# Expert layer in five pieces whose first steps alternate with the last slots of the context attention

## What is computed

```python
x = _layernorm(x + _L1_xattn_ref(x, ctx_2048, mask_BxSxS2_ff0, ...))
x = _layernorm(x + _L1_ffn_ref(x, L1_ffn_router_w, L1_ffn_down_w, L1_ffn_up_w))
# _L1_ffn_ref
logits = jnp.einsum('bth,eh->bte', x, router_w)          # 8 experts
weights = jax.nn.softmax(logits, axis=-1)
top_w, top_idx = jax.lax.top_k(weights, K)               # K = 2
gate = weights * topk_mask
a = silu(jnp.einsum('bth,eih->beti', x, down_w))         # 16 per expert
out = jnp.einsum('beth,bte->bth', einsum('beti,ehi->beth', a, up_w), gate)
```

## Time and profile before

| | us |
|---|---|
| median of 3 runs | 2366.31 |
| lowest and highest | 2366.27, 2366.6 |
| span of the profiled execution | 2368.8 |
| busy in the span: PE, DVE, ACT, POOL | 2103.1, 1295.4, 1062.5, 822.0 |

### The profile page before, as it was taken

How to read it: one execution, slowest core, us unless ns; L and a number is a source line. 1 busy time by engine, 2 the same in 40 slices (tenths; PEclk the granted TensorE clock), 3 DMA queues, 4 the chain that set the end, 5 groups by cost and what they waited for, 6 DMA issues and landing times.

```text
span 2368.8 us, 37759 instructions
## 1 busy us (share of the span) xinstructions
PE 2103.1 (89%) x13655; PEld 1671.4 (71%) x13669; DVE 1295.4 (55%) x3333; ACT 1062.5 (45%) x2367; POOL 822.0 (35%) x836
## 2 busy tenths in 40 slices
PE   7899999899999978999999999969999778888764
PEld 6688888687877866877777888756555366666542
DVE  2454445544455456545456411356777676777655
ACT  3332333444444424444534222146666547777632
POOL 1753444334343322134441135264535231322100
PEclk9899999899999998999999999979999789999986
DMA  3302102012012012011110012033324210000001
GB/s 125 135 32 67 45 32 76 19 41 65 28 45 65 19 36 72 25 53 37 41 48 25 32 40 80 1 56 55 62 44 63 94 33 28 15 19 6 1 10 71
DMA packets 57879, 109.04 MB, mean 46 GB/s; under 512 B 7136, under 2 KB 35040, under 8 KB 54112
## 3 DMA queue, kind: packets, MB, share of 16 engines
q1 hardware_dynamic: 57696, 106.63, 15.8%
HBM read 86.10 MB, written 4.26 MB: 38 GB/s over the span
## 4 chain that ended last, share of the span: by engine, by line
PE 40%; DVE 10%; issue 7%; ACT 4%; POOL 2%; DMA 1%; SPq 1%; ACTq 0%; DVEq 0%; POOLq 0%
PE PS L1293 17%; PE PS L1790 3%; PE PS L1886 3%; PE PS L1309 2%; DVE st L191 2%; ACT xP L2551 1%; DVE aM L2026 1%; PE PS L1854 1%; PE PS L956 1%; PE PS L1874 1%; PE PS L968 1%; DVE PS L2673 1%; PE PS L1841 1%; ACT xN L240 1%; PE PS L1897 1%
## 5 line engine op out<-in xcount | busy, mean ns | idle before, releaser
L1293 PE MATMUL PS<-WH,bXH 128*128 128x512 f32 x640 | 258.4, 404 | 0.0
L1293 PE MATMUL PS<-WH,bXL 128*128 128x512 f32 x640 | 250.2, 391 | 0.0
L1293 PE MATMUL PS<-WL,bXH 128*128 128x512 f32 x640 | 250.2, 391 | 0.0
L2026 DVE TENSOR_REDUCE aM<-PS 128x4 f32<-128x1024 f32 x128 | 153.8, 1221 | 55.2 <-PE PS L1854 54.0
L384 PE MATMUL PS<-aXH,QKH 128*128 128x512 f32 x384 | 157.4, 410 | 15.6 <-ACT sq L597 7.8
L1595 POOL TENSOR_TENSOR WL<-sg,WH 128x512 fp32r<-128x512 f32 x80 | 102.0, 1306 | 181.7 <-ACT WH L1409 181.7
L1590 POOL TENSOR_TENSOR mixed<-mixed,s 128x256 f32<-128x256 f32 x112 | 82.5, 740 | 233.9 <-DVE s L1491 233.8
L384 PE MATMUL PS<-aXL,QKH 128*128 128x512 f32 x384 | 152.7, 398 | 0.0
L384 PE MATMUL PS<-aXH,QKL 128*128 128x512 f32 x384 | 152.7, 398 | 0.0
L1965 ACT ACTIVATE aPT<-PS 128x1024 f32<-128x1024 f32 x128 | 128.8, 1024 | 50.3 <-PE PS L1874 49.4
L684 DVE TENSOR_TENSOR qkL<-PS,qkH 128x512 fp32r<-128x512 f32 x96 | 65.9, 690 | 142.7 <-ACT qkH L561 142.7
(11 more groups left out here) (395 smaller groups left out, 6048.2 us busy)
## 6 DMA issues: line engine op xcount, KB each, us to landing
sg<-in_gu SPq DMA_DIRECT2D x16, 1024.0 KB, 4.9
gQK<-in_Wqk SPq DMA_DIRECT2D x16, 768.0 KB, 6.2
gC<-in_Wc SPq DMA_DIRECT2D x16, 512.0 KB, 6.9
lgB<-gate_sums SPq DMA_DIRECT2D x32, 256.0 KB, 4.5
aqs<-aQH SPq DMA_DIRECT2D x64, 128.0 KB, 4.3
xN<-in_xT SPq DMA_DIRECT2D x4, 1024.0 KB, 12.0
xN<-in_x SPq DMA_DIRECT2D x4, 1024.0 KB, 7.5
cst<-in_cT SPq DMA_DIRECT2D x8, 512.0 KB, 3.8
```

The lines of the kernel that those rows point to most:

```text
L1293: mm = e.matmul(PS[:, b, :], x[:, kc, c:c + 128], y[:, kc, :], start=kc == 0 and n == 0, stop=kc == KC - 1 and n == 2)
L2026: e.tensor_reduce(M[j % 2][:, :, :].rearrange("x q (h c) -> x h q c", h=2)[:, :, :, i], PS[:, b:b + 2, :].rearrange("p h (q k) -> p h q k" ...
```

## The change

Slots stay as they are, and the list becomes a list of slots, so that each engine stops after every slot. The experts are written as ticks on the same count: ticks 50 to 86. From slot 50 on every engine does one slot of the context attention and then the tick of the experts with the same number; ticks 75 to 86 follow the last slot, 74. The experts now have five pieces, of tiles 0 to 3, 4 to 7, 8 to 11, 12 and 13, 14 and 15, which start at ticks 55, 60, 65, 70 and 75 and have twelve steps r of one tick each: 0 and 1 transposes and splits, 2 logits, 3 logits back, hidden values and activation, 4 softmax of the gates, 5 choice, 6 gates transposed, 7 spread, product and split, 8 and 9 output and addition, 10 and 11 norm and store. Each piece makes its own gates. The SiLU of ACT is now half a tanh on ACT (L2985 in the new numbering) and one more DVE operation (L3032), with the factor one half in the spreading matrix. The weights are loaded at tick 50 and split at ticks 53 and 54, and lie in places that the context attention no longer needs. The norm of tiles 8 to 11 is moved from slots 62 to 69 to slots 59 to 62; tiles 12 and 13 are normed in slots 67 to 69 and tiles 14 and 15 in slot 74, as last parts of the list. The four banks of the scores are given to the others after the last exponential.

```diff
@@ Places.__call__
-        n = 4
+        n = 2 if dt == BF16 else 4
@@ cross1
-        if j % 2 and j < 7:
-            for i, what in zip((22, 23, 26, 29), ("n1", "n2", "n3", "n4")):
+        if j % 2 and j < 7 or j >= 6:
+            for i, what in zip({5: (19, 20, 21, 22), 6: (19, 20, 20, 21), 7: (18, 18, 18, 18)}.get(j, (22, 23, 26, 29)), ("n1", "n2", "n3", "n4")):
                 put(base + i, 3, what, j)
-    plan = [what for slot in sorted(at) for _, _, what in sorted(at[slot], key=lambda x: x[:2])]
+    first, last = min(at), max(at) + 1
+    plan = [[what for _, _, what in sorted(at.get(slot, ()), key=lambda x: x[:2])] for slot in range(first, last)]
...
+    spans = {1: range(0, 4), 3: range(4, 8), 5: range(8, 12), 6: range(12, 14), 7: range(14, 16)}
+    for t in range(NT):
+        K.tx[t] = (o_add.upto(t + 1),)
+    norms = {j: Norm(K, tiles, False) for j, tiles in spans.items()}
...
-    norms[7] = Norm(K, range(12, 16), True)
-    rooms = dict(R.of)
-    K.rooms = Rooms()
...
+                    if (j, i) == (7, 7):
+                        R.give("scores", 4, s_exp.upto(8 * J))
@@ experts1
+    pieces = [range(0, 4), range(4, 8), range(8, 12), range(12, 14), range(14, 16)]
+    starts = [55, 60, 65, 70, 75]
+    P, first, last = len(pieces), 50, starts[-1] + 12
...
+    norms = [Norm(K, tiles, True, space=1) for tiles in pieces]
+    def steps(tick):
+        for p in range(P):
+            if 0 <= tick - starts[p] < 12:
+                yield p, tick - starts[p]
...
     def scalar(e):
+        for tick in range(first, last):
+            if tick == 53:
+                e.wait_ge(*K.keys_made)
+                e.wait_ge(*in_w.upto(1))
+                e.activation(WH[:, :, :], wst[:, :, :], ACTF.Copy).then_inc(w_hi.sem, 1)
+                e.wait_ge(*in_u.upto(1))
+                e.activation(UH[:, :], ust[:, :], ACTF.Copy).then_inc(w_hi.sem, 1)
+            for p, r in steps(tick):
+                n, wide = len(pieces[p]), 128 * len(pieces[p])
+                if r in (0, 1):
+                    for kc in (2 * r, 2 * r + 1):
...
+                elif r == 3:
+                    if p:
+                        e.wait_ge(*h_out.upto(p))
+                    e.wait_ge(*h_mm.upto(p + 1))
+                    e.activation(ht[:, 0:wide], PS[:, rooms["f_hidden", p][0], 0:wide], ACTF.Tanh,
+                                 scale=0.5).then_inc(h_act.sem, 1)
+                elif r == 4:
+                    e.wait_ge(*g_in.upto(p + 1))
+                    e.activation(gt[:, 0:n, :], gt[:, 0:n, :], ACTF.Exp).then_inc(g_exp.sem, 1)
...
+                elif r == 11:
+                    norms[p].apply_act(e)
-            e.activation(ha[:, p, :], PS[:, rooms["hidden", p][0], :], ACTF.Silu).then_inc(h_out.sem, 1)
...
     def vector(e):
+        for tick in range(first, last):
+            if tick == 54:
+                e.wait_ge(*w_hi.upto(2))
+                e.tensor_tensor(WL[:, :, :], wst[:, :, :], WH[:, :, :].bitcast(F32), ALU.subtract).then_inc(w_lo.sem, 1)
+                e.tensor_tensor(UL[:, :], ust[:, :], UH[:, :].bitcast(F32), ALU.subtract).then_inc(w_lo.sem, 1)
+            for p, r in steps(tick):
+                n, wide = len(pieces[p]), 128 * len(pieces[p])
+                if r in (0, 1):
+                    for kc in (2 * r, 2 * r + 1):
+                        e.wait_ge(*x_hi.upto(4 * p + kc + 1))
+                        e.tensor_tensor(XL[:, kc, 0:wide], PS[:, rooms["f_turn", p, kc][0], 0:wide],
+                                        XH[:, kc, 0:wide].bitcast(F32), ALU.subtract).then_inc(x_lo.sem, 1)
+                elif r == 2:
+                    if p:
+                        e.wait_ge(*l_turn.upto(p))
+                    e.wait_ge(*l_mm.upto(p + 1))
+                    e.tensor_copy(lT[:, 0:wide], PS[0:8, rooms["f_logits", p][0], 0:wide]).then_inc(l_out.sem, 1)
+                elif r == 3:
+                    lgt = PS[:, rooms["f_logits_turned", p][0], 0:8 * n].rearrange("p (a c) -> p a c", a=n)
+                    if p:
+                        e.wait_ge(*t_mm.upto(p))
...
+                    e.wait_ge(*h_act.upto(p + 1))
+                    e.scalar_tensor_tensor(out=ha[:, 0:wide], in0=ht[:, 0:wide], scalar=1.0,
+                                           in1=PS[:, rooms["f_hidden", p][0], 0:wide], op0=ALU.add,
+                                           op1=ALU.mult).then_inc(h_out.sem, 1)
+                elif r == 4:
+                    e.wait_ge(*g_exp.upto(p + 1))
+                    step(e.tensor_reduce(rm[:, 0:n, 0], gt[:, 0:n, :], AX.X, ALU.add))
+                    step(e.reciprocal(rm[:, 0:n, :], rm[:, 0:n, :]))
+                    step(e.tensor_tensor(gt[:, 0:n, :], gt[:, 0:n, :], rm[:, 0:n, :].broadcast_to([128, n, 8]), ALU.mult))
...
+                elif r in (8, 9):
+                    for t in pieces[p][2 * (r - 8):2 * (r - 8) + 2]:
+                        for w in came[t]:
+                            e.wait_ge(*w)
+                        e.wait_ge(*o_mm.upto(t + 1))
+                        e.tensor_tensor(xN[:, t, :], PS[:, rooms["f_out", t][0], :], xN[:, t, :],
+                                        ALU.add).then_inc(o_add.sem, 1)
+                elif r == 10:
+                    norms[p].stats(e, step)
+                    norms[p].seed(e, step)
+                elif r == 11:
+                    norms[p].newton(e, step)
@@ decoder
-        order += [(i, 1) for i in range(4, 7)]
+        order += [(4, 1), (5, K.own_slots - K.first_slot)]
+        for slot in range(K.own_slots, K.past_slots):
+            order += [(5, 1), (6, 1)]
+        order += [(6, e1.ticks - (K.past_slots - K.own_slots))]
```

More of the change, by code:

```diff
@@ L2409, in tensor @@
+        for slot in plan:
+            for what, j, i in slot:
+                y = j % 2
+                if what == "weight":
+                    b, left = rooms["w", i]
                     for w in left:
                         e.wait_ge(*w)
-                    e.wait_ge(*r_rnd.upto(2 * j + a + 1))
+                    e.wait_ge(*w_rnd.upto(i + 1))
                     for c in range(KC):
-                        mm = e.transpose(PS[:, b, 128 * c:128 * c + 128], qr[4 + a][:, 128 * c:128 * c + 128], idF[:, :])
@@ L2471, in tensor @@
+                        mm = e.transpose(PS[:, b, 128 * c:128 * c + 128], weight(i)[0][:, 128 * c:128 * c + 128], idF[:, :])
+                    mm.then_inc(w_mm.sem, 1)
+                elif what in ("weights_out", "scale"):
+                    key = "scale_o" if what == "weights_out" else ("scale", j)
+                    n = nth_scale.index("o" if what == "weights_out" else j) + 1
+                    b, left = rooms[key]
                     for w in left:
                         e.wait_ge(*w)
-                    e.wait_ge(*a_out.upto(4 * j + 4))
@@ L2497, in scalar @@
+            yield
     def scalar(e):
@@ L2901, in tensor, with ready @@
+    def tensor(e):
+        def ready(key):
+            b, left = rooms[key]
             for w in left:
                 e.wait_ge(*w)
[L2903 to L2910 removed]
@@ new lines, in gpsimd @@
+    def gpsimd(e):
+        step = K.steps(e, "pool_step")
+        for tick in range(first, last):
+            if tick == 53:
+                e.wait_ge(*K.keys_made)
+                step(e.memset(R8[:, :], 0.5))
+                step(e.affine_select(out=R8[:, :], in_=R8[:, :], compare_op=ALU.is_ge, fill=0.0, base=0,
+                                     pattern=[[1, 128]], channel_multiplier=-16))
+                e.affine_select(out=R8[:, :], in_=R8[:, :], compare_op=ALU.is_ge, fill=0.0, base=15,
+                                pattern=[[-1, 128]], channel_multiplier=16).then_inc(r8.sem, 1)
+            yield
@@ new lines, in sync @@
+    def sync(e):
+        for tick in range(first, last):
+            if tick == first:
+                for w in K.context_read:
+                    e.wait_ge(*w)
+                e.dma_start(wst[:, :, :], d["fw"]).then_inc(in_w.sem, 16)
+                e.dma_start(ust[:, :], d["fu"]).then_inc(in_u.sem, 16)
+            for p, r in steps(tick):
+                if r == 11:
+                    t0, t1 = pieces[p][0], pieces[p][-1] + 1
+                    e.wait_ge(*norms[p].done.upto(len(pieces[p])))
+                    e.dma_start(out[:, t0:t1, :], xN[:, t0:t1, :]).then_inc(stored.sem, 16)
+            if tick == last - 1:
+                e.wait_ge(*stored.upto(P))
+            yield
@@ L3097, in beside @@
+    K.own_slots = first
+    return Stage(last - first, banks, tensor, scalar, vector, gpsimd, sync)
 def beside(order, s, pieces, t, groups):
@@ L3117, in decoder @@
         K.rooms, rooms = Rooms(), K.rooms
-        rest = [whole(stage(K)) for stage in (attention1, cross1, experts1)]
-        stages = [first, a0, c0, e0, *rest]
+        a1 = whole(attention1(K))
+        x1 = cross1(K)
+        e1 = experts1(K)
+        stages = [first, a0, c0, e0, a1, x1, e1]
         A, C, X = 1, 2, 3
```

1335 lines of the change are left out of this document (623 added, 712 removed).

## The result

| | before | the change |
|---|---|---|
| median, us | 2366.45 | 2386.6 |
| lowest and highest of four | 2366.27, 2367.89 | 2379.12, 2387.86 |
| profiled execution: time, span | 2368.8 (span) | 2385.55, 2383.8 |

The ratio is 1.0069, 95% interval 1.0056 to 1.0082: slower by 13 to 19 us. Timed a second time (run `e8_change_again`) it was 1.006, 1.0047 to 1.0072. The forecast was 9.9 slower, 2376 in a range from 2356 to 2390.

The account below looks back on a forecast made before the run. A loop of waits, not any engine's work, was taken to bound the kernel. 26 us lost in the rounds and 45.6 in the other slots against 61.8 won gave 2366.3 + 9.9 = 2376.2, say 2376 us, range 2356 to 2390.

Parts of the forecast that it names:

- Sign and mechanism: Whole kernel: 9.9 us slower, since next-slot maxima on DVE stand behind expert steps waiting for PE and ACT; chance 0.55.
- The rounds: Last context block, four rounds from scores to exponentials (slots 55 to 63): 62.95 us against 38.0, last exponential 26.1 later.
- The rest of the slots: Slots 63 to 74, following DVE's queue: work 48.7 plus waits 15.8, 64.5 us, from 2270.7 to 2335.2.
- the application with the high parts: Rest of the slots: DVE's low parts wait for two ACT norm applications and the high parts behind, 7.7 us.
- hidden values and tanh: Rest of the slots: DVE waits three times for hidden product and tanh, 5.5 us.
- the spread and `aH`: Rest of the slots: DVE waits for the gates' spread and the high parts `aH`, 2.6 us.
- Ticks 75 to 86: Experts' ticks after the last slot: 39.8 us along DVE and its waits, then 3.7 for the last store.
- From profile to median: Whole kernel: median taken 2.5 us below the profiled span, so 2366.3 + 9.9 = 2376.2.
- C: Rival, whole kernel: more loss, DVE-POOL collisions or PSUM banks cost 9 us more, 2385; chance 0.15.
- 26 lost in the rounds, 45.6 in the rest, 61.8 won: Forecast's balance: 26 us lost in rounds, 45.6 in the remaining slots, against 61.8 won after them.
- A: Rival: experts' products keep PE at 2.4 GHz, saving about 5.5, 4 and 2.5 us, so 2364; chance 0.15.
- B: Rival: the loop's idle time absorbs expert steps, rounds lose 8.6 instead of 26.1, under 12 us each, 2358.7; chance 0.15.

Follow-up runs that it names:

- e4: The change with starts 56, 62, 66, 70, 75 and DVE's part of transposes, logits and hidden steps one tick later: 2369.34 us, 1.0001 of the kernel before.
- e2: The change with pieces starting at ticks 64, 69, 74, 79, 84, behind the rounds: 2383.08 us, 1.0058 of the kernel before.
- e7: The change with starts 56, 62, 67, 71, 75, DVE a tick later in piece 0 and piece 1's transposes, ACT's norm applications last: 2355.36 us, 0.9945 of before.
- e5: The change with ACT's expert norm applications put last within each tick: 2368.21 us, 0.9999 of the kernel before.
- e9: The change with ACT's expert norm applications last in the tick, timed again on another chip: 2368.66 us, 1.0004 of the kernel before.

## Why the prediction was right, and where it was not

**Sign and mechanism: right.** Slower, by a wait that takes the place of the one removed: an expert step goes PE, ACT, DVE in one tick, and the maxima of the next slot stand behind it. e4 takes these waits away and the rounds fall, while the granted clock in them rises from 0.85 to 0.93.

**The rounds: right.** (The terms of round 1 add up to 14.85, not 14.95.) Forecast 14.95, 15.75, 15.45 and 16.8, measured 14.0, 16.1, 15.0 and 16.4; last exponential forecast at 2271.8, measured 2270.7.

**The rest of the slots: the term that failed.** The waits in it were put too low. Forecast 64.5 from DVE's last maxima, work 48.7 and waits 15.8, to the end of the last context norm at 2335.2; it ended at 2341.1, 71.7 after maxima that were 1.3 early, and the last addition of the context attention ended at 2333.8 instead of 2327. DVE's work was less, 44.9, its idle time more, 26.6:

```profile
2269.60:2341.10 71.50, 45.03 (x195) 27.71 (x195) 44.91 (x152) 18.06 (x38) 6.44 (x6) 0.75 0.07 30
```

Of the waits I had named, the application with the high parts came out at 3.94 + 3.73 = 7.7 (forecast 7.7), hidden values and tanh at 3.10 + 1.26 (5.5), the spread and `aH` at 3.0 (2.6). Not named at all: DVE's additions that wait for output products, 3.38 and four small ones, 4.9 in sum; copies of logits, 2.27 and 0.40; a scaling, 1.36. These are 8.9 of the 10.8 by which the idle time exceeds my 15.8, and the work, 3.8 less than forecast, hides a third of them in the sum. The 3.38 comes from PE, which waited 2.64 for a bank that ACT's copy of the transposed had to free:

```profile
2271.64 0.79 PE L2958 MATMUL PS<-UH,aH 128*128 128x512 f32 x1 [2.64 <-ACT xPT L2572]
```

I had put banks at nothing but for one value product. And the application's price was right for what I asked of it, DVE's stand at the low parts, but it is not what the application costs: gates and logits behind it come late too, and taking it out of the way is worth 13.4.

**Ticks 75 to 86: right.** Forecast 39.8 and 3.7, together 43.5; measured 42.7. The last application ends at 2380.8, and DMA issues after 2341 show why the store was shorter than 3.7:

```profile
out<-xN SPq DMA_DIRECT2D x2, 512.0 KB, 2.6
```

**From profile to median.** Against the profiled executions the change is 2383.8 - 2368.8 = 15.0 slower; forecast 9.9: the rest of the slots was put 7.2 too low, what lies ahead of it 1.3 and what follows 0.8 too high. I had carried over that before's median lay 2.5 below its profiled span; the change's lay 2.8 above its own. That made 15.0 into 20.1, in the second measurement 13.4. All runs with both numbers take 1.7 us or more longer than their span, so the profiled execution of the kernel before, 2368.8, was itself some 4 above its median, and the change's, 2385.55, 1 below. The 2386.6 lies at what I had given for C, but not by C's cause.

**"26 lost in the rounds, 45.6 in the rest, 61.8 won": right as a sum, misleading as a cause.** It suggests that the rounds' loss is to be avoided by starting later. e2 does that and gains little or nothing (1.0058 against 1.0069 and 1.006); the work only moves.

**The rivals.** A, PE stays fast: refuted for the change, the granted clock is 0.83 from 2200 to 2240 and 0.80 from there to 2265 (0.87 and 0.84 before), with products at either level, and 0.70 behind. By the rule of the Trainium skill that I cited (TensorE: Matmul & The Clock Gate, "HAM oscillation — how this bites in real kernels") the slow terms stay, and the trace agrees. In the rounds of e4 and e7, where DVE's part comes a tick later, the granted clock is 0.93 and 0.92. B, the loop absorbs the steps: refuted in round 1, 14.0 instead of under 12; it is half true of e4 and e7, where the rounds are 43.7 and 45.6. C, collisions: two, as far as the timelines show. One step was drawn out to 0.37 at 2249.86, beside POOL's rounding (0.19 at 2287.67), and one to 1.26 instead of 0.16 at 2319.30, beside POOL's addition:

```profile
2249.86 0.37 DVE L3048 SCALAR_TENSOR_TENSOR gt<-fpq,gt 128x32 f32<-128x32 f32 x1
```

```profile
2319.28 1.26 POOL L2769 TENSOR_TENSOR xN<-xoN,xN 128x512 f32<-128x512 f32 x1 [10.29 <-DVE xoN L2710]
```

```profile
2319.30 1.26 DVE L211 SCALAR_TENSOR_TENSOR nb<-na,nv 128x4 f32<-128x4 f32 x1
```

Together they are 1.3 us, about as much as the one collision of before, and the 9 us would have needed eight like the second. The rule of the Trainium skill on GpSimd and DVE that I cited (SBUF — State Buffer, "Who interferes with whom") bears on the places where they meet; the trace agrees, both steps have two SBUF inputs, and the second ends with the addition beside it.

## What to carry to other kernels

When stages are interleaved by ticks, look at each tick for a step whose engines wait for each other within it, and give the last engine of it one tick more, where the PSUM banks can be held that long: the work is the same, and what stands behind it waits less. In every queue put what nobody waits for last, and price it not only by the engine that stands behind it but by all that stands behind the same place. And if undoing an overlap gains nothing, the overlap isn't worthless yet: it may be paying a wait that can be taken away by itself.

## What was not expected of the hardware

The same kernel at the same place had TensorE at either level of its clock. e5 and e9 are one program, and e5's profiled execution takes 2374.9, 6 more than e9's 2369.1. The busy time of e5 between 2290 and 2310 and then of e9:

```profile
2290.00:2310.00 20.00, 18.93 (x73) 11.40 (x72) 15.06 (x43) 7.15 (x13) 1.36 (x2) 0.71 0.13 54
```

```profile
2290.00:2310.00 20.00, 14.51 (x66) 8.70 (x65) 17.99 (x53) 6.56 (x12) 1.36 (x2) 0.93 0.13 53
```

The granted clock is 0.71 against 0.93. Two of the twelve logits products of piece 2 in e5:

```profile
2297.78 0.63 PE L2922 MATMUL PS<-fXH,fWH 128*8 128x512 f32 x1
2298.21 0.63 PE L2922 MATMUL PS<-fXL,fWH 128*8 128x512 f32 x1
```

and in e9:

```profile
2294.07 0.39 PE L2922 MATMUL PS<-fXH,fWH 128*8 128x512 f32 x1
2294.30 0.40 PE L2922 MATMUL PS<-fXL,fWH 128*8 128x512 f32 x1
```

They follow 0.43 apart at 1.2 GHz and 0.23 at 2.4 GHz. Over eleven executions of e9 the mean granted clock lies between 0.948 and 0.957 and the time between 2374.9 and 2365.6, the slower ones at the lower clock. What tips it one way or the other in one program stays open. So one profiled execution can miss a kernel's median by 6 us, and a median less a profiled span is no constant to carry over to another kernel.
